# A transformer block on one core: weights by head in 32-partition copies, a second issuing queue, new orders of the prelude, and seventeen idle transposes

## The reference

```python
x = x + _L0_xattn_ref(_layernorm(x), ctx_1024, ctx_1024, mask, Wq, bq, Wk, bk, Wv, bv, Wo, bo)
x = x + _L0_attn_ref(_layernorm(x), W_Q, W_K, W_V, W_O)
x = x + _L0_ffn_ref(_layernorm(x), router_w, w0_kernel, w1_kernel, wo_kernel)

def _L0_xattn_ref(query, key, value, mask, Wq, bq, Wk, bk, Wv, bv, Wo, bo):
    Q = query @ Wq.T + bq; K = key @ Wk.T + bk; V = value @ Wv.T + bv   # split in 16 heads
    energy = einsum('bhqd,bhkd->bhqk', Q, K) / sqrt(16)
    energy = where(mask == 0, -1e20, energy)
    x = einsum('bhqk,bhkd->bhqd', softmax(energy), V)
    return x @ Wo.T + bo
```

## Time and profile before

| | us |
|---|---|
| median of 3 runs | 530.65 |
| lowest and highest run | 529.42, 531.2 |
| the profiled execution | 530.13 |
| its span in the trace | 528.2 |
| PE busy | 497.9 (94% of the span) |
| DVE, ACT, GpSimd busy | 389.5, 336.5, 269.7 |
| start of the first energies (batch 0) | 28.75 |
| start of the energies of batch 1 | 38.49 |

### The profile page before, as it was taken

The page is one execution under the profiler, slowest core; times in us unless marked ns, Lnnn a source line. Parts: engine busy times, 40 slices in busy tenths (PEclk is TensorE's granted clock), DMA queues, the critical chain, the costliest instruction groups (busy, mean ns, idle before and its releaser), DMA issues.

```text
span 528.2 us, 18602 instructions
## 1 busy us (share of the span) xinstructions
PE 497.9 (94%) x6784; PEld 459.1 (87%) x6784; DVE 389.5 (74%) x962; ACT 336.5 (64%) x865; POOL 269.7 (51%) x363
## 2 busy tenths in 40 slices
PE   1899999999999999999999989999999999999996
PEld 0778888798888898888878868999999999999995
DVE  2546456676676767666678868999999999999963
ACT  1457776676676667675773789666666666666640
POOL 4126345436434364444433364766676766767650
PEclk9979999999999999999999999999999999999998
DMA  6612221211111121110006300556565635656202
GB/s 176 198 46 54 47 49 24 54 43 47 29 45 34 34 50 21 50 40 2 3 4 201 122 1 2 175 153 230 168 192 166 200 127 195 206 157 200 79 1 79
DMA packets 58126, 48.92 MB, mean 93 GB/s; under 512 B 20942, under 2 KB 49744, under 8 KB 58064
## 3 DMA queue, kind: packets, MB, share of 16 engines
q1 hardware_dynamic: 58064, 48.09, 31.1%
HBM read 46.86 MB, written 1.08 MB: 91 GB/s over the span
## 4 chain that ended last, share of the span: by engine, by line
PE 86%; DVE 5%; issue 4%; ACT 3%; DMA 2%; SPq 1%; DVEq 0%; ACTq 0%; POOL 0%
PE bank L225 21%; PE bank L227 19%; PE bank L226 19%; PE bank L638 6%; PE bank L614 4%; PE bank L662 4%; PE bank L571 2%; PE bank L945 2%; PE bank L1058 2%; DMA w_raw<-in_L_xattn_Wk 2%; PE bank L800 2%; ACT Pr L1128 1%; PE bank L762 1%; ACT PTd L1247 1%; PE bank L773 1%
## 5 line engine op out<-in xcount | busy, mean ns | idle before, releaser
L225 PE MATMUL bank<-XT_lo,W_hi 128*128 128x256 f32 (+1 forms) x352 | 99.5, 283 | 0.2 <-issue 0.2
L226 PE MATMUL bank<-XT_hi,W_lo 128*128 128x256 f32 (+1 forms) x352 | 99.0, 281 | 0.0
L227 PE MATMUL bank<-XT_hi,W_hi 128*128 128x256 f32 (+1 forms) x352 | 98.8, 281 | 0.0
L2146 POOL TENSOR_TENSOR W_lo<-raw,W_hi 128x256 fp32r<-128x256 f32 (+1 forms) x88 | 89.2, 1013 | 7.1
L2040 POOL TENSOR_TENSOR Pr<-Pr 128x1024 f32<-128x1024 f32 x31 | 58.8, 1898 | 47.5 <-DVE Pr L1515 46.8
L1128 ACT ACTIVATE Pr<-Sc,nmax 128x257 f32<-128x257 f32 x128 | 63.9, 502 | 20.8 <-DVE nmax L1506 20.8
L1506 DVE CUSTOM_DVE_ANT_0 Sc<-bank,mask_add 128x257 f32<-128x257 f32 x128 | 47.0, 423 | 40.1 <-PE bank L614 17.9
L1969 DVE TENSOR_TENSOR hid_lo<-hid,hid_hi 128x256 fp32r<-128x256 f32 (+1 forms) x88 | 72.9, 829 | 1.5 <-ACT hid_hi L1411 1.5
L1937 DVE TENSOR_TENSOR W_lo<-raw,W_hi 128x512 fp32r<-128x512 f32 (+1 forms) x88 | 68.8, 783 | 5.3 <-ACT W_hi L1323 1.5
L2144 POOL CAST W_hi<-raw 128x256 fp32r<-128x256 f32 (+1 forms) x88 | 40.9, 464 | 51.2 <-PE bank L227 35.5
L225 PEld LDWEIGHTS bank<-XT_lo,W_hi 128*128 128x128 f32 (+1 forms) x352 | 65.4, 186 | 0.4 <-issue 0.4
(11 more groups left out here) (250 smaller groups left out, 1372.1 us busy)
## 6 DMA issues: line engine op xcount, KB each, us to landing
raw<-in_L_ffn_w_kernel SPq DMA_DIRECT2D x32, 512.0 KB, 4.6
ctx_raw<-in_ctx SPq DMA_DIRECT2D x32, 256.0 KB, 2.8
raw<-in_L_ffn_wo_kernel SPq DMA_DIRECT2D x16, 512.0 KB, 5.7
raw<-in_L_ffn_w_kernel SPq DMA_DIRECT2D x16, 344.0 KB
last_prob<-Pr SPq DMA_DIRECT2D x128, 1.0 KB
raw<-in_L_ffn_wo_kernel SPq DMA_DIRECT2D x8, 256.0 KB
x_sb<-in_x SPq DMA_DIRECT2D x4, 256.0 KB, 6.1
VL_all<-vl_rows SPq DMA_DIRECT2D x8, 128.0 KB
```

Source lines behind the costliest of these rows:

```text
L225: pe.matmul(dst, a_hi, b_lo, start=first, stop=False)
L226: pe.matmul(dst, a_lo, b_hi, start=False, stop=False)
L227: return pe.matmul(dst, a_hi, b_hi, start=False, stop=last)
L2146: po.tensor_tensor(W2_lo[0:w, m % RW, :], raw2[0:w, t, :], f(W2_hi[0:w, m % RW, :]), ALU.subtract)\
```

## The change

1. A by-head weight is loaded in four copies of 32 partitions x 2 x 256 in place of two of 128 partitions x 256. The bytes and their places are the same.
2. SP issues x before Wq. Wk and the three biases are issued by ACT, ahead of its table load. The second half of x goes ahead of the mask.
3. `idle` is defined earlier, and PE makes 14 idle transposes before Wq's transposes and 3 between Wq's and Wk's.
4. `kl` moves ahead of Wv and the queries, and waits only for the slots that it needs. The wait for all of ACT's copies moves from before the energies of batch 0 to before its values.
5. DVE normalises the tokens before it makes Wk's low half, makes `lastT`'s before the context's, the second statistics before Wv's, and the second half of the tokens before the low half of context 1.
6. GpSimd's two memsets for the self attention move ahead of both `rstd`. Its first `spread` waits for the queries, which are now last.

```diff
-    slots = [("w", 0), ("w", 1), ("bias", 0), ("lastT", 0), ("xT", 0), ("xT", 1), ("w", 2), ("q", 0), ("q", 1), ("kl", 0), ("vl", 0)]
+    slots = [("w", 0), ("w", 1), ("bias", 0), ("lastT", 0), ("xT", 0), ("xT", 1), ("kl", 0), ("w", 2), ("q", 0), ("q", 1), ("vl", 0)]
...
-            src = weights[i].rearrange("(r c x) n -> c r x n", r=HG, c=KH)
-            for c in range(KH):
-                eng.dma_start(w_raw[:, i, c, :], src[c]).then_inc(w_in[i], 16)
+            src = weights[i].rearrange("(r c x) n -> r x c n", r=HG, c=KH)
+            for r in range(HG):
+                eng.dma_start(w_raw[r * S:(r + 1) * S, i, :, :], src[r]).then_inc(w_in[i], 16)
...
-        load_weight(sp, 0)
         load_x(0)
         load_x(1)
-        load_weight(sp, 1)
...
+        load_weight(sp, 0)
...
             elif kind == "kl":
-                pe.wait_ge(sm["first_act"], n)
-                pe.wait_ge(sm["first_dve"], sum(by_dve[:n]))
+                pe.wait_ge(sm["first_act"], slot("lastT", 0) + 1)
+                pe.wait_ge(sm["first_dve"], sum(by_dve[:slot("lastT", 0) + 1]))
...
-        for n in range(2):
-            prepare(n)
+        idle(14, bk[5])
+        prepare(0)
+        idle(3, bk[5])
+        prepare(1)
         turn_ctx(0, 0, 16)
...
-        pe.wait_ge(sm["first_act"], NS)
-        pe.wait_ge(sm["first_dve"], sum(by_dve))
+        pe.wait_ge(sm["first_act"], slot("q", 1) + 1)
...
                 if isinstance(j, int) and b == 0:
+                    pe.wait_ge(sm["first_act"], NS)
                     values(0, 0)
...
     @block_.scalar
     def _(ac):
+        load_weight(ac, 1)
...
         statistics(0)
         low(slot("w", 0))
+        norm_tokens(0)
         low(slot("w", 1))
-        norm_tokens(0)
+        low(slot("lastT", 0))
         split_ctx(0, 0)
-        low(slot("lastT", 0))
         low(slot("xT", 0))
         low(slot("xT", 1))
+        statistics(1)
         low(slot("w", 2))
-        statistics(1)
         set_mask()
+        norm_tokens(1)
         split_ctx(1, 1)
-        norm_tokens(1)
```

More of the change, by code:

```diff
@@ L275, in weight_in @@
     def weight_in(i):
-        return 16 * KH if i in BY_HEAD else 16
+        return 16 * HG if i in BY_HEAD else 16
     def front(t):
@@ L383, in load_x @@
             sp.dma_start(x_sb[:, 2 * i:2 * i + 2, :], x_v[:, 2 * i:2 * i + 2, :]).then_inc(x_in[i], 16)
-        load_weight(sp, 0)
         load_x(0)
         load_x(1)
-        load_weight(sp, 1)
-        for i, vec in enumerate((xbq, xbk, xbv)):
-            if i < 2:
-                src = vec.rearrange("(r c x) -> c r x", r=HG, c=KH)
-                dst = bias_raw[KH * i:KH * i + KH, :].rearrange("c (r x) -> c r x", r=HG)
-            else:
-                src, dst = vec.rearrange("(k p) -> k p", p=P), bias_raw[KH * i:KH * i + KH, :]
-            sp.dma_start(dst, src).then_inc(sm["bias_in"], 16)
+        load_weight(sp, 0)
         def first_ctx(b):
@@ L430, in _ @@
         first_ctx(1)
+        load_x(2)
+        load_x(3)
         for h in range(HG):
             sp.dma_start(mask_i[h * S:(h + 1) * S, :], mask[0, 0]).then_inc(sm["mask_in"], 16)
-        load_x(2)
-        load_x(3)
         first_ctx(2)
@@ L490, in _, with idle @@
         pe.wait_ge(sm["const_in"], 16)
+        def idle(n, into):
+            for _ in range(n):
+                pe.transpose(into[:, 0:P], ident, ident)
         def prepare(n):
@@ L524, in prepare @@
             elif kind == "vl":
-                pe.wait_ge(sm["first_act"], n)
-                pe.wait_ge(sm["first_dve"], sum(by_dve[:n]))
+                pe.wait_ge(sm["first_act"], slot("w", 2) + 1)
+                pe.wait_ge(sm["first_dve"], sum(by_dve))
                 for k in range(KH):
@@ L832, in logits @@
             last.then_inc(sm["c_logits_made"], 1)
-        for n in range(2):
-            prepare(n)
+        idle(14, bk[5])
+        prepare(0)
+        idle(3, bk[5])
+        prepare(1)
         turn_ctx(0, 0, 16)
-        for n in range(2, slot("w", 2) + 1):
+        for n in range(2, slot("kl", 0) + 1):
             prepare(n)
         keys(0, 0)
-        for n in range(slot("q", 0), slot("vl", 0)):
+        for n in range(slot("w", 2), slot("vl", 0)):
             prepare(n)
@@ L940, in turn_weights_of @@
             last.then_inc(sm["ct_made"], 1)
-        def idle(n, into):
-            for _ in range(n):
-                pe.transpose(into[:, 0:P], ident, ident)
         y_, z = TT - 2, TT - 1
@@ L1063, in _ @@
     def _(ac):
+        load_weight(ac, 1)
+        for i, vec in enumerate((xbq, xbk, xbv)):
+            if i < 2:
+                src = vec.rearrange("(r c x) -> c r x", r=HG, c=KH)
+                dst = bias_raw[KH * i:KH * i + KH, :].rearrange("c (r x) -> c r x", r=HG)
+            else:
+                src, dst = vec.rearrange("(k p) -> k p", p=P), bias_raw[KH * i:KH * i + KH, :]
+            ac.dma_start(dst, src).then_inc(sm["bias_in"], 16)
         def prepare(n):
@@ L1262, in _ @@
         split_ctx(0, 0)
-        for n in range(2, slot("w", 2) + 1):
+        for n in range(2, slot("kl", 0)):
             prepare(n)
         ac.wait_ge(sm["first_act"], slot("bias", 0) + 1)
+        prepare(slot("kl", 0))
         keep_keys(0, 0)
-        for n in range(slot("q", 0), slot("vl", 0)):
+        for n in range(slot("w", 2), slot("vl", 0)):
             prepare(n)
@@ L1985, in _ @@
         po.memset(V[:, :, :, :, :], 0.0).then_inc(sm["v_zero"], 1)
+        po.memset(PTd[:, :, :, :, :], 0.0)
+        po.memset(Vm[:, :, :, :], 0.0).then_inc(sm["diag_zero"], 1)
         po.wait_ge(sm["ones_set"], 1)
@@ L1990, in _ @@
             po.tensor_tensor(rstd[:, tiles], mv[:, tiles, 1], half[:, tiles], ALU.pow).then_inc(sm["ln1_rstd"], 1)
-            if part == 0:
-                po.memset(PTd[:, :, :, :, :], 0.0)
-                po.memset(Vm[:, :, :, :], 0.0).then_inc(sm["diag_zero"], 1)
         po.wait_ge(sm["table_in"], 16)
-        po.wait_ge(sm["first_act"], slot("kl", 0) + 1)
+        po.wait_ge(sm["first_act"], slot("q", 1) + 1)
         def add_bias(u):
```

## The result

| | before | after |
|---|---|---|
| median, us | 530.11 (529.42 to 531.2, 4 runs) | 515.67 (515.43 to 516.76, 4 runs) |
| profiled execution, us | 530.13 | 515.45 |
| its span, us | 528.2 | 513.6 |
| energies of batch 0, us | 28.75 | 19.62 |
| energies of batch 1, us | 38.42 | 27.42 |

The ratio of the changed kernel to the one before is 0.973 (95%: 0.9706 to 0.9754). The forecast was 519.2 us with a range of 517.0 to 525.0; the time lies 1.3 us under its low end. A second session gave 516.77 us (515.57 to 519.87, 6 runs) beside 529.87 for the kernel before, a ratio of 0.9747 (0.9714 to 0.978). All ten runs of the changed kernel have the median 516.2, and with that the experiments are compared.

The account below looks back on a forecast made before the run. PE, 94% busy, bounds the kernel, with a prelude made long by weight loads and a low clock. Prelude 9.85 plus first batch 1.7 gave 11.5 us off 530.13, so 518.6, plus 0.5 for the median: 519.2 us, range 517.0 to 525.0.

Parts of the forecast that it names:

- Landing of the weights: Prelude: Wq landed and turned from 5.9 us, Wk no longer awaited until 12.88; some 7 of the 9.85 us.
- Rival 3: Prelude: new copies still on few engines, Wq landing at 7 to 8, or PE's clock falling before 38; about 524; chance 0.07.
- The volume term: Prelude loads: 64 KB table and 1024 KB of x, Wq, Wk at 370 GB/s, 3.0 us from 1.7; landed by 5.2.
- The clock: Prelude and batch 0: idle transposes bring PE's rise to 7.7 to 8.7 instead of 21.2; some 3 of the 9.85 us.
- Rival 1: Prelude: transposes do not raise the clock, rise at about 17, energies at 22; 522.1, or 523.9 with slow first batch; chance 0.17.
- Rival 2: Prelude loads: SP's and ACT's issues exclude each other, Wq lands at 7.8, clock rises late; 522.1; chance 0.08.
- Rival 4: Self attention's eight W_Q and W_K copies delay batch 4's context; no loss up to 1.56 us per copy; slower, chance 0.02.
- Rival 5: Later batches: no change, if they had slack to eat the prelude's gain; chance 0.04.

Follow-up runs that it names:

- no_idles: The changed kernel without the 14 and the 3 idle transposes: 520.24 us, ratio 0.9803 to the kernel before.
- old_copies: The changed kernel with the old two copies of 128 partitions per by-head weight: 521.93 us, ratio 0.986 to the kernel before.
- filled: The changed kernel with 17 idle transposes in front, 3 behind Wq's and 3 more before the token transposes: 519.0 us, ratio 0.9773.
- front17: The changed kernel with all 17 idle transposes ahead of Wq's and none behind: 516.15 us, ratio 0.9721.
- only_idles: The kernel before with only the 14 and 3 idle transposes added: 528.26 us, ratio 0.9963.
- tail_idles: The changed kernel with 12 more idle transposes before the last product: 517.0 us, ratio 0.9737; a second profile's single run 515.35.
- front11: The changed kernel with 11 idle transposes in front instead of 14, the 3 behind Wq's kept: 515.63 us in one run.
- front14: The changed kernel with the 14 idle transposes in front but without the 3 behind Wq's: 516.85 us, ratio 0.9755.
- only_copies: The kernel before with only the by-head weights in four copies of 32 partitions: 526.29 us, ratio 0.9928.
- before_three: The kernel before with only three idle transposes between Wq's and Wk's: 530.76 us in one run.
- before_tail: The kernel before with only 12 idle transposes ahead of the final combination: 528.45 us in one run.

## Why the prediction was right and where it failed

**The step that failed** is the sentence "from then on the batches are alike and PE-bound, and the change does not touch them", with the zero that it gave to everything behind batch 1. The batches are not alike: two of those between 1 and 14 held a stand of 1.1 to 1.3 us, and with the change both are gone. They do no work that the change touches; what goes with them is when blocks of instructions are fetched. That is 2.2 us in the first pair and 2.7 in the second. The fall of the clock at the end adds 0 to 1.5 us by chance. With the two stands of the first pair taken off, 519.2 would have been 517.0, the low end, and 515.5 with the end at the high clock as well. That this comes so near 515.67 is in part luck: the place of the change itself gave 11.0 us in one pair and 9.8 in the other, where the forecast had 11.5.

**Landing of the weights: right in kind, 1.2 us short.** Wq was turned at 7.07 in place of 5.9; the second profile and no_idles have 7.4. Rival 3's place would have been 7 to 8, but the DMA engines were full, not few. The volume term was mis-sized. It had 1.1 MB at 370 GB/s, done at 4.7 (5.2 with the landing). The engines moved 305 GB/s from 3 to 6 us and reached 1.13 MB at 5.87, and by 7.03, when Wq had landed, they had moved 1.45 MB: what is issued behind Wq shared the engines with it. The table landed 2.4 us after its issue, against 1.8 in the earlier trace rows, and so the idle transposes began at 3.21 and not at 2.54. That the new copies use more engines is seen in the windows of old_copies and after, 0.67 and all of the engines' time; the rule of the Trainium skill ("DMA: Bandwidth & Descriptors", section on why a DMA increments its semaphore by 16) agrees with it, but no row has such a copy alone on all 16.

**The clock: right in kind, late by 2 to 4 us, and it cost less than that.** The rise came at 10.9 and at 12.7 us in the two profiles, 7.7 and 9.5 after the first transpose, in place of 5.2 to 6.2. Since DVE sets `kl` (filled), only 0 to 1 us of this reached the energies: the prelude gave 9.13 and 8.41 us in place of 9.85. That the high level lasts through batch 0 was right: 7.80 us in both profiles, 8.0 forecast, and ACT's copies of KT are the last piece there, as forecast.

**Rival 1 is refuted.** front17 and only_idles turned Wq at the high pace with nothing but transposes of the identity before, and in the changed kernel and old_copies the tokens' transposes went at it from 10.9 and 16.4 us, ahead of the first real product. The Trainium skill ("TensorE: Matmul & The Clock Gate", Part 4: PE-mode transpose) has it that the high clock does not engage for transposes; here they raised it. The kernel before spoke for the rival less than was said: its real products began at 18.52, 2.7 us ahead of the rise and not 2.3. What a late rise costs is seen in no_idles: energies at 23.64, where the rival had 22, and yet 520.24 us, where it had 522.1. The rise came even later than the rival had it, and the difference lies behind batch 1, where one stand was gone and the last product ran at the high clock.

**Rival 2 is refuted** by the rows of issues, which overlap. **Rival 4** had its price in them too: W_Q's four copies 1.88 us, 0.47 each, under the 1.56 from which something is lost. Rival 5 held nothing.

**The parts do not add up**, and the forecast had them as one chain for this reason. Copies alone give 4.1 us and idle transposes alone 1.4 to 2.0 (by the medians, by the ratio), of which about one is a stand. Leaving one part out of the whole costs 5.7 (copies), 4.0 (transposes), 6.3 (orders), 4.6 (queue): 20.6 us in sum, out of 14. Each part removes what would be late next when another one is in place.

**What is left open.** Which rule ties the program to the places of its blocks. In batches 9 and 13 the stands came again, or stayed away again, whenever the same program was profiled twice (before, after, tail_idles). But the blocks do not come at fixed times: near batch 9 at -0.49 us in one profile of after and at -1.38 in the other, near batch 29 at 1.04 and -0.29, and there the stand of 0.88 us was in the first alone. So chance has a part in it. front11 and front14 have equally many instructions and differ, and tail_idles differs from after only behind batch 31. Which of the orders (`kl`, the token tiles, the memsets) gives what part of the 6.3 us was not tested either.

## What to carry to other kernels

When a change shortens one place, compare the starts of all later repetitions, not only the end: an offset that jumps in one of them is a cause of its own, and "issue" behind a half-made burst of small instructions is what to look for. Cost the edits of a prelude as one chain, since removing the first wait shows only what is late second. A span from one execution carries the chances of that execution (here 1.5 us at the end), so set a row that differs only there aside before explaining it.

## What the runs showed of the hardware

- Transposes of the identity raise PE's clock: eight weight transposes in 1.09 us (front17) against four in 1.12.
- PE can stay at the low level for some 12.6 us of gapless work (no_idles, 7.4 to 20.0), and had fallen by 12.7 after gaps of 0.76 us near 9.2 and 0.17 at 11.2 (front17). When it rises differs between two executions of one program: 10.9 and 12.7 us.
- PE stood for 0.9 to 1.6 us within 64 products of 32 columns, 0.75 us of work, in the 19 cases in which a block of 16 KB of instructions was fetched 0.2 to 0.8 us ahead of them in batches 9 and 13. The same instructions in later passes of the loop, without a fetch, never stood. In this kernel that is 1.0 to 1.5 us for each time, 0.2 to 0.3% of the whole, and it came and went with edits far away, though not with all of them (only_copies, before_three and before_tail kept both).
- A DVE tile of 0.40 us took 2.22 beside two memsets of GpSimd (only_copies).
- Two queues issue at the same time: four copies in 1.91 us on ACT, while SP issued three others and began the next; SP's four of Wq took 1.89 (after).
